# Two extra products of constants ahead of each pair of gathered tiles in the second gather's loop

## The chip, the cores and the metric

One NeuronCore of a Trainium2 chip runs the whole kernel as one launch. The metric is the device time of one execution in microseconds (us). The engines are named as in the profile: PE is the matrix engine (PEld its weight loads), DVE the vector engine, ACT the scalar engine, POOL the GpSimd engine that issues the gathers, and SP the sync engine. A difference of under 2% is about what a measurement of this kernel can't tell from no change.

## The reference, cut to what matters

```python
N_NODES, N_EDGES, D = 6250, 100000, 256
h    = layernorm(x) @ W.T                   # (6250, 256)
msgs = edge_weight[:, None] * h[dst]        # one row of 256 for each edge
x    = x + segment_sum(msgs, src, 6250)     # graph part: the gathers
x    = x + moe_ffn(layernorm(x))            # 16 experts, the best 2 of each node, F = 512
```

The edges come in the order of `dst`, so the kernel has to sort them by `src`, the node that a message is summed into. It sums the normalized rows first and multiplies the sums by W afterwards.

## The kernel before

The 6250 nodes are taken as 49 windows of 128 rows. The edges are sorted by window into tiles of 128 edges. For a tile, POOL gathers 128 rows of 256 numbers from DRAM (`xn_rows`) into SBUF by an indirect DMA, DVE builds a 128-wide table `picks` that holds each edge's weight in the column of its node, and PE multiplies the two, which adds the tile's messages to the window's sum in a PSUM bank.

There are two gathers. The first takes 4 tiles for each window (`fbuf`, lines L737, L1095, L1261) while the sort of the edges goes on. The second, which the change touches, takes the rest, in pairs of tiles:

- POOL (`gather_gpsimd`, L470) gathers a pair as two indirect DMAs of 128 rows into one of 16 places of `hbuf`. It needs the rows' numbers (`ix`, which DVE writes for half a ring, 8 pairs, at a time, L420, semaphore `ix_set`) and a free place (`used`, which PE raises).
- DVE (`gather_vector`, L491) builds `picks` for a pair, twice 128x256, in one of two buffers. It waits until PE has used the pair before last (`used`). At the third pair of each half ring it writes the numbers of the next half ring, and that releases POOL's next 16 gathers.
- SP (`gather_sync`, L456 to L458) waits for each pair's `picks` and for its gathers, and raises `pair_in`.
- PE (`gather_tensor`, L549) waits for `pair_in` and makes the pair's two products of 256 columns in fp32. Each is two MATMUL and two LDWEIGHTS records in the trace. `quad` does two pairs; `window` runs it in a loop over the window's quads, in which `used` is raised, and once more after the loop for the quad that the window shares with the next, in which it isn't: the next window begins with that same quad. Behind it come the transposes of the window before (`turn`, L558), the multiplication by W (`project`, L565 to L567) and the sum that the first gather left (L581), which opens the next window. ACT copies each closed window out (`agg`, L627) and works on the projected rows (L609 to L621).

After the gathers come the routing and the expert layers on all engines (from 1820 us on in the trace), and a last normalization. In them PE works with the same banks, after the gathers' end. Bank 6 is used by nothing in the second gather.

What each line does in the loop is seen in the code. `s` counts pairs, `q` is the window's bank and half of `picks`:

Of the kernel before, what the change touches and what calls it, by code (L numbers as in the profile page):

```python
# [18 lines left out]
def await_turn(engine, sem, turn, per, value):  # L19

    if isinstance(turn, int):
        if per * turn + value > 0:
            engine.wait_ge(sem, per * turn + value)
    else:
        engine.wait_ge(sem, turn * per + value)


def gnn_moe_kernel(nc, x, src, dst, edge_weight, gnn_w, gate_w, gate_b, w1, b1, w2, b2, gamma, beta, out):
# [4 lines left out]
    P = 128  # L33
# [62 lines left out]
    with ctx:  # L96
        def sb(name, shape, dt):
            return ctx.enter_context(nc.sbuf_tensor(name, shape, dt))

        def bank(name, shape, dt=fp32):  # L100
            return ctx.enter_context(nc.psum_tensor(name, shape, dt))
# [5 lines left out]
        ident = sb("ident", [P, P], fp32)  # L107
        iota_i = sb("iota_i", [P, P], i32)
        iota_two = sb("iota_two", [P, 2 * P], fp32)
# [176 lines left out]
        bk = [bank(f"bank{i}", [P, 512]) for i in range(8)]  # L286
# [140 lines left out]
        def window_pairs(engine, window):  # L427
            for w in range(4):
                window(w, w % 2)
            with engine.Fori(2, NW // 2) as i:  # L430
                window(i * 2, 0)
                window(i * 2 + 1, 1)
            window(NW - 1, 0)
# [107 lines left out]
            choose(SOON[1], NW)  # L541

        def gather_tensor(pe):
            def quad(s, q):
                place = s & (PR - 1)
                for j in range(2):
                    pe.wait_ge(pair_in, s + j)
                    for k in range(2):
                        m = nc.tensor.matmul(bk[q][:, 0:D], picks[:, j, k, q * P:(q + 1) * P],  # L549
                                             hbuf[:, ds(place + j, 1), k, :].rearrange("p s d -> p (s d)"),  # L550
                                             start=False, stop=False, skip_group_check=True)
                    yield m

            def turn(w, q):
                pe.wait_ge(agg_ready, w + 1)
                await_turn(pe, aggT_ready, w, 1, -1)
                for b in range(NB):
                    s = nc.tensor.transpose(bk[2 + q][:, b * P:(b + 1) * P], agg[q][:, b * P:(b + 1) * P], ident[:])  # L558
                s.then_inc(agg_turned, 1)

            def project(w, q):
                pe.wait_ge(aggT_ready, w + 1)
                await_turn(pe, x1_added, w, 1, -1)
                for b in range(NB):
                    nc.tensor.matmul(bk[4 + q][:, 0:D + EX], aggT[q][:, b, :], wT[:, b, :], start=b == 0, stop=False, skip_group_check=True)  # L565
                nc.tensor.matmul(bk[4 + q][:, D:D + EX], ident[:], raw[:, ds(w, 1), :].rearrange("p w e -> p (w e)"), start=False, stop=False, skip_group_check=True)
                s = nc.tensor.matmul(bk[4 + q][:, 0:D], ident[:], x1[:, ds(w, 1), :].rearrange("p w d -> p (w d)"), start=False, stop=True, skip_group_check=True)  # L567
                s.then_inc(projected, 1)

            def window(w, q):  # L570
                first = pe.value_load(quad_i[0:1, ds(w, 1)], min_val=1, max_val=TT // 2)
                end = pe.value_load(quad_i[0:1, ds(w + 1, 1)], min_val=3, max_val=TT // 2)
                if isinstance(w, int) and w == 0:
                    pe.wait_ge(rows_in[0], 32)
                if isinstance(w, int) and 2 <= w < 4:
                    for t in range(w - 1, WT - 1) if w == 3 else (1,):
                        pe.wait_ge(rows_in[t], 32)
                    if w == 3:
                        pe.wait_ge(rows_in[WT - 1], 48)
                await_turn(pe, agg_ready, w, 1, -1)  # L580
                nc.tensor.matmul(bk[q][:, 0:D], ident[:], first_sums[:, ds(w, 1), :].rearrange("p w d -> p (w d)"), start=True, stop=False, skip_group_check=True)  # L581
                with pe.Fori(first, end, 2) as s:
                    for m in quad(s, q):
                        m.then_inc(used, 1)

                for m in quad(end, q):
                    pass
                m.then_inc(closed, 1)
                if not isinstance(w, int) or w >= 1:
                    turn(w - 1, 1 - q)  # L590
                if not isinstance(w, int) or w >= 2:
                    project(w - 2, q)

            pe.wait_ge(tables_ready, FBLK + TBLK)
            pe.wait_ge(first_summed, NW)
            pe.sem_inc(used, PR)
            window_pairs(pe, window)

            pe.wait_ge(closed, NW)
            pe.sem_inc(used, 2 * PR)  # L600
            turn(NW - 1, 0)
            project(NW - 2, 1)
            project(NW - 1, 0)
# [1324 lines left out]
```

## Time and profile before

| | |
|---|---|
| time, median of 3 runs | 2383.14 us (2364.69 to 2874.64) |
| time of the profiled execution | 2405.79 us |
| its span, first to last instruction | 2404.0 us |
| granted PE clock over the span | 0.787 of 2.4 GHz |
| second gather, 625 to 1820 us | 1195 us |
| PE busy in it | 641.0 us, at a granted clock of 0.74 |
| POOL busy in it | 614.9 us, 640 gathers |

The second gather is half of the span. A granted clock of 0.74 is a mean over stretches at 1.2 GHz (0.5) and stretches at 2.4 GHz (1.0). No engine is busy for more than 54% of this half, so the time lies in what they wait for from each other.

### The profile page before, as it was taken

How to read it: one execution, taken by the hardware profiler on the slowest of the kernel's cores; microseconds unless marked ns; L12 is line 12 of the kernel's file. 1: busy time of each engine (PE TensorE's matmuls, PEld its weight loads, DVE VectorE, ACT ScalarE, POOL GpSimd, SP SyncE). 2: the span in 40 equal slices, each digit the busy share in tenths (PEclk: the TensorE clock that was granted, in tenths of full speed). 3: DMA queues.
4: the chain of work that ended last, by engine and by line, in shares of the span. 5: the costliest groups of instructions: out<-in, count | busy, mean ns of one | idle time of the engine just before them, and what ended most of it. 6: DMA issues, size and time to landing. Idle time of an engine off the chain costs nothing. (4 is left out here: it accounts for less than half of the span.)

```text
span 2404.0 us, 33977 instructions
## 1 busy us (share of the span) xinstructions
PE 1508.3 (63%) x7875; PEld 1206.6 (50%) x7876; DVE 970.1 (40%) x2547; ACT 645.8 (27%) x1788; POOL 1204.3 (50%) x1170
## 2 busy tenths in 40 slices
PE   5256977564445565555565546464644799998975
PEld 3245866452334343333343434343433799897864
DVE  7995799472112222222222132121317333332338
ACT  5741266330000110101010100101015344443456
POOL 0045558786655555555555444545552355454434
PEclk9595589686668676877677767677876999999988
DMA  4112212224522222222222222222236222224346
GB/s 154 62 54 82 77 52 66 72 66 142 179 79 72 70 70 70 70 70 70 70 70 70 70 61 65 72 66 74 72 70 190 86 71 77 94 85 159 118 145 229
DMA packets 121466, 215.63 MB, mean 90 GB/s; under 512 B 21001, under 2 KB 82756, under 8 KB 121281
## 3 DMA queue, kind: packets, MB, share of 16 engines
q0 software_dynamic: 52864, 140.45, 19.9%
q1 hardware_dynamic: 53664, 56.14, 7.0%
q10 hardware_dynamic: 14880, 18.35, 2.3%
q8 instruction: 26, 0.43, 0.1%
q14 instruction: 32, 0.25, 0.0%
HBM read 172.32 MB, written 42.54 MB: 89 GB/s over the span
## 5 line engine op out<-in xcount | busy, mean ns | idle before, releaser
L470 POOL DMA_INDIRECT hbuf<-xn_rows,ix x640 | 614.9, 961 | 574.2 <-DVE ix L420 217.8
L549 PE MATMUL bank<-hbuf,picks 128*128 x1640 | 535.1, 477 | 549.8 <-SPq L458 274.4
L549 PEld LDWEIGHTS bank<-hbuf,picks 128*128 128x128 f32 x1640 | 363.6, 237 | 714.1 <-issue 660.4
L491 DVE TENSOR_SCALAR picks<-iota_two,marks 128x256 f32<-128x256 f32 x640 | 239.5, 420 | 920.6 <-remote 616.4
L737 POOL DMA_INDIRECT fbuf<-xn_rows,first_tables x196 | 230.1, 1174 | 130.0 <-PE bank L1261 66.9
L627 ACT ACTIVATE agg<-bank 128x256 f32<-128x256 f32 x49 | 18.8, 385 | 863.3 <-PE bank L549 565.5
L1845 PE MATMUL bank<-rowsT,w_sb 128*128 128x128 f32 x1744 | 216.3, 278 | 19.1 <-issue 19.1
L1845 PEld LDWEIGHTS bank<-rowsT,w_sb 128*128 128x128 f32 x1744 | 212.2, 193 | 31.0 <-issue 26.3
L1855 PE MATMUL bank<-w_sb,hT 128*128 128x256 f32 x872 | 209.2, 382 | 0.9 <-ACT hT L1803 0.6
L1781 POOL DMA_INDIRECT expert_out<-y_sb,to_i x112 | 111.4, 995 | 192.6 <-DVE y_sb L1890 188.0
L1279 PE MATMUL bank<-work 128*128 128x192 bf16 x1568 | 154.8, 254 | 75.2 <-DVE work L1067 57.1
L1279 PEld LDWEIGHTS bank<-work 128*128 128x128 bf16 x1568 | 137.8, 99 | 97.8 <-issue 95.1
L1803 ACT ACTIVATE hT<-bank,b_cols 128x128 f32<-128x128 f32 x436 | 139.6, 366 | 164.4 <-PE bank L1845 152.6
L1261 PE MATMUL bank<-fbuf,x 128*128 128x256 f32 x392 | 149.2, 506 | 48.9 <-DMA fbuf<-xn_rows,first_tables 22.9
L1855 PEld LDWEIGHTS bank<-w_sb,hT 128*128 128x128 f32 x872 | 157.6, 191 | 20.1 <-ACT hT L1803 2.7
L726 POOL DMA_INDIRECT edge_groups<-recs,dest_i x56 | 85.2, 1521 | 162.1 <-DVE recs L1074 143.2
L1771 POOL DMA_INDIRECT xt<-xn_rows,from_i x116 | 112.9, 973 | 68.6 <-issue 36.7
L1261 PEld LDWEIGHTS bank<-fbuf,x 128*128 128x128 f32 x392 | 84.5, 246 | 68.8 <-issue 34.8
L1890 DVE TENSOR_TENSOR y_sb<-bank,b_b 128x256 f32 x109 | 46.3, 425 | 167.0 <-PE bank L1855 162.2
L1095 DVE TENSOR_SCALAR x<-iota_two,first_tables 128x128 f32<-128x128 f32 x196 | 65.2, 367 | 119.2 <-PE bank L1261 53.2
L1067 DVE TENSOR_TENSOR work<-work,tables 128x768 bf16<-128x768 bf16 (+2 forms) x176 | 95.5, 599 | 5.6
L1051 DVE TENSOR_TENSOR work<-iota_rows,low_i 128x512 bf16<-128x512 bf16 (+2 forms) x136 | 95.1, 749 | 0.2 <-DVE tables L1146 0.2
(293 smaller groups left out, 1729.0 us busy)
## 6 DMA issues: line engine op xcount, KB each, us to landing
w_sb<-in_L_ffn_w_dram ACTq DMA_DIRECT2D x28, 512.0 KB
hbuf<-xn_rows,ix POOLq DMA_INDIRECT x640
first_sums<-x SPq DMA_DIRECT2D x49, 128.0 KB
first_sums_back<-first_sums SPq DMA_DIRECT2D x7, 896.0 KB
xn_rows<-xn SPq DMA_DIRECT2D x7, 896.0 KB, 4.6
x<-in_x_dram SPq DMA_DIRECT2D x6, 896.0 KB
ya<-expert_out SPq DMA_DIRECT2D x5, 896.0 KB, 5.3
yb<-expert_out SPq DMA_DIRECT2D x5, 896.0 KB, 7.2
```

Of the source, the lines that this page charges most:

```text
L470: pool.indirect_dma_start(hbuf[:, 1 + j, k, :], None, xn_dram, bass.IndirectOffsetOnAxis(ap=ix[:, 2 * j + k:2 * j + k + 1], axis=0)).then_ ...
L491: s = v.tensor_scalar(picks[:, j % 2, k, :], iota_two[:], marks[:, 0, 2 * j + k:2 * j + k + 1], marks[:, 1, 2 * j + k:2 * j + k + 1], ALU. ...
L549: m = nc.tensor.matmul(bk[q][:, 0:D], picks[:, j, k, q * P:(q + 1) * P], hbuf[:, ds(place + j, 1), k, :].rearrange("p s d -> p (s d)"), st ...
L737: pool.indirect_dma_start(fbuf[:, s % RH, :], None, xn_dram, bass.IndirectOffsetOnAxis(ap=fdst_i[:, s:s + 1], axis=0)).then_inc(xn_gathere ...
L1067: s = v.tensor_tensor(fields[n % RM][:, h0:h1, :, :, :], colhot[n % RJ][:, h0:h1, None, :, :].to_broadcast(shape), pieces[:, e0 + h0:e0 + ...
L1261: nc.tensor.matmul(bk[w % 2][:, 0:D], fpicks[:, used % RK, :], fbuf[:, used % RH, :], start=t == 0, stop=t == FT - 1).then_inc(first_used, 1)
L1279: s = nc.tensor.matmul(sums_at[c % 2][h][:, 0:2 * PIECES * SP_], rowhot[n % RP][:, k // 2, h * P:(h + 1) * P, k % 2], fields[n % RM][:, k ...
L1771: pool.indirect_dma_start(xt[:, k, :], None, xn2_dram, bass.IndirectOffsetOnAxis(ap=from_i[:, k:k + 1], axis=0)).then_inc(xt_in[k], 16)
L1781: pool.indirect_dma_start(y_dram, bass.IndirectOffsetOnAxis(ap=to_i[:, k:k + 1], axis=0), y_sb[:, k % 2, :], None).then_inc(y_sent[k], 16)
L1803: act.activation(hT[:, f, :], bk[f][:, 0:P], ACT.Relu, bias=b1_cols[:, ds(e * FB + f, 1)]).then_inc(hT_ready, 1)
L1845: m = nc.tensor.matmul(bk[f][:, 0:P], w1_sb[:, q, b, f * P:(f + 1) * P], rowsT[:, b, :], start=b == 0, stop=b == NB - 1)
L1855: m = nc.tensor.matmul(bk[5][:, 0:D], hT[:, f, :], w2_sb[:, q, f, :], start=f == 0, stop=f == FB - 1)
```

## The change

Inside the loop over a window's quads, and not in the quad behind it, PE makes two further products for each pair, after its wait for `pair_in` and ahead of the pair's own two. Both multiply the identity by `iota_two`, a constant of 256 columns, in fp32, into bank 6. Nobody reads that bank, and no semaphore is raised by them.

```diff
-            def quad(s, q):
+            def quad(s, q, kept_busy):
                 place = s & (PR - 1)
                 for j in range(2):
                     pe.wait_ge(pair_in, s + j)
+                    if kept_busy:
+                        for k in range(2):
+                            nc.tensor.matmul(bk[6][:, 0:2 * P], ident[:], iota_two[:], start=True, stop=True)
                     for k in range(2):
                         m = nc.tensor.matmul(bk[q][:, 0:D], picks[:, j, k, q * P:(q + 1) * P],
...
-                    for m in quad(s, q):
+                    for m in quad(s, q, True):
                         m.then_inc(used, 1)
 
-                for m in quad(end, q):
+                for m in quad(end, q, False):
                     pass
```

PE is the only engine whose instructions change. This is its queue from the first window's opening sum through one turn of the loop, before. A REGISTER_ALU on line 549 carries the wait for `pair_in`, and the ISA rows set up addresses:

```order
L581 MATMUL bank<-first_sums_back,ident 128x256
L582 UNCONDITIONAL_BRANCH
L549 REGISTER_ALU
L549 ISA
L549 MATMUL bank<-hbuf,picks 128x256
L549 ISA
L549 MATMUL bank<-hbuf,picks 128x256
L547 REGISTER_ALU
L549 ISA
L549 MATMUL bank<-hbuf,picks 128x256
L549 ISA
L549 MATMUL bank<-hbuf,picks 128x256
```

The same place now. Lines from 547 on have moved down by three:

```order
L584 MATMUL bank<-first_sums_back,ident 128x256
L585 UNCONDITIONAL_BRANCH
L550 MATMUL bank<-iota_two,ident 128x256 x2
L552 REGISTER_ALU
L552 ISA
L552 MATMUL bank<-hbuf,picks 128x256
L552 ISA
L552 MATMUL bank<-hbuf,picks 128x256
L547 REGISTER_ALU
L550 MATMUL bank<-iota_two,ident 128x256 x2
L552 ISA
L552 MATMUL bank<-hbuf,picks 128x256
```

The two products stand at the head of each pair, and now the first of them carries the wait for `pair_in`. The address instructions come behind them.

## Rows read from the trace of the kernel before

**Rows 1.** The page's head: busy time, share of the span, instructions.

```profile
span 2404.0 us, 33977 instructions
PE 1508.3 (63%) x7875; PEld 1206.6 (50%) x7876; DVE 970.1 (40%) x2547; ACT 645.8 (27%) x1788; POOL 1204.3 (50%) x1170
```

**Rows 2.** Windows: three stages; columns in the first row.

```profile
core 0: us, PE busy (x) PEld busy (x) DVE busy (x) ACT busy (x) POOL busy (x), PEclk, DMA share, GB/s
0.00:625.00 625.00, 384.80 (x2515) 312.39 (x2516) 449.26 (x1005) 261.76 (x608) 320.65 (x273) 0.75 0.29 89
625.00:1820.00 1195.00, 641.00 (x2228) 456.62 (x2228) 265.64 (x732) 114.20 (x441) 614.88 (x640) 0.74 0.25 71
1820.00:2404.00 584.00, 482.48 (x3132) 437.62 (x3132) 255.18 (x813) 269.86 (x739) 268.72 (x257) 0.93 0.39 128
```

**Rows 3.** Groups by line: busy us, mean ns, then idle before, by releaser.

```profile
L470 POOL DMA_INDIRECT hbuf<-xn_rows,ix x640 | 614.9, 961 | 574.2 <-DVE ix L420 217.8 <-issue 197.7 <-PE bank L549 158.4
L549 PE MATMUL bank<-hbuf,picks 128*128 x1640 | 535.1, 477 | 549.8 <-SPq L458 274.4 <-issue 273.5
L491 DVE TENSOR_SCALAR picks<-iota_two,marks 128x256 f32<-128x256 f32 x640 | 239.5, 420 | 920.6 <-remote 616.4 <-PE bank L549 246.2 <-issue 44.4
```

**Rows 4.** Timeline, POOL, 1209 to 1263 us: gathers at bursts' starts and ends.

```profile
1209.49 0.95 POOL L470 DMA_INDIRECT hbuf<-xn_rows,ix  x1 [14.23 <-DVE ix L420]
1210.74 1.04 POOL L470 DMA_INDIRECT hbuf<-xn_rows,ix  x1 [0.30 <-issue]
...
1228.46 0.96 POOL L470 DMA_INDIRECT hbuf<-xn_rows,ix  x1 [0.30 <-issue]
1234.55 0.95 POOL L470 DMA_INDIRECT hbuf<-xn_rows,ix  x1 [5.13 <-DVE ix L420]
```

**Rows 5.** Timeline, ACT and DVE, the same stretch.

```profile
1230.40 0.38 ACT L627 ACTIVATE agg<-bank 128x256 f32<-128x256 f32 x1 [22.00 <-remote]
1232.77 0.73 DVE L491 TENSOR_SCALAR picks<-iota_two,marks 128x256 f32<-128x256 f32 x2 [15.84 <-remote]
1233.42 0.17 DVE L420 COPY ix<-tables 128x16 int32 x1
```

**Rows 6.** Timeline, PE, the same stretch: runs of records, start and length.

```profile
1211.24 1.99 PE L549 MATMUL bank<-hbuf,picks 128*128 x8 [0.40 <-SPq L458]
1213.75 1.99 PE L549 MATMUL bank<-hbuf,picks 128*128 x8 [0.52 <-issue]
1216.41 1.99 PE L549 MATMUL bank<-hbuf,picks 128*128 x8 [0.67 <-issue]
1218.23 0.38 PE L558 MATMUL bank<-ident,agg 128*128 128x128 f32 x2
...
1224.65 2.07 PE L549 MATMUL bank<-hbuf,picks 128*128 x4 [1.44 <-issue]
1233.79 6.08 PE L549 MATMUL bank<-hbuf,picks 128*128 x16 [7.08 <-SPq L458]
```

**Rows 7.** Windows on `hbuf`, pauses between bursts: PE, PEld, POOL busy, clock, DMA.

```profile
1195.30:1209.50 14.20, 9.64 (x27) 6.99 (x28) 0.01 (x1) 0.70 0.03 10
...
1229.40:1234.50 5.10, 0.71 (x2) 0.63 (x3) 0.02 (x1) 0.50 0.09 29
...
1254.50:1262.70 8.20, 4.03 (x11) 3.18 (x12) 0.02 (x1) 0.54 0.06 16
...
1282.80:1291.10 8.30, 5.56 (x15) 4.09 (x16) 0.00 (x0) 0.61 0.06 16
...
1311.00:1320.80 9.80, 7.73 (x19) 5.54 (x20) 0.00 (x0) 0.54 0.05 14
...
1340.90:1355.70 14.80, 8.19 (x24) 5.90 (x25) 0.02 (x1) 0.67 0.03 9
```

**Rows 8.** Source L549: durations in ns, min/median/max, first and last start.

```profile
L549 PE MATMUL bank<-hbuf,picks x1640: 379/379/792, 631.7 to 1811.6; 128*128 x183
```

**Rows 9.** Timeline, first gather, 599 to 618 us, PE and DVE.

```profile
599.73 5.85 PE L1261 MATMUL bank<-fbuf,x 128*128 128x256 f32 x18 [1.60 <-DVE x L1095]
618.03 0.35 DVE L1095 TENSOR_SCALAR x<-iota_two,first_tables 128x128 f32<-128x128 f32 x1 [11.91 <-PE bank L1261]
```

## The prediction

> **What bounds the kernel now.** I read the stages first, then the second gather by lines, then one turn of its ring in time. The stage that the change touches runs from 625 to 1820 us, 1195 of 2404 us [rows 1, 2]. Nothing is saturated in it: PE is busy for 641 us, POOL for 615, DVE for 266 [rows 2]. So the question is what each waits for. POOL sat idle for 574 us ahead of its 640 gathers: 198 us of it are "issue", the 0.30 us between two gathers, and 218 + 158 = 376 us are waits for the row numbers that DVE writes and for places that PE frees [rows 3].
>
> In time this is a ring with two phases. POOL gets 8 pairs' numbers at once and issues 16 gathers 1.26 us apart, so a burst takes 20 us (1209.5 to 1229.4). Then it pauses until DVE writes the next numbers (1233.42) and starts again at 1234.55 [rows 4, 5]. The 640 gathers make 40 such groups of 16, the first two in one go, so there are 38 pauses. The 376 us over 38 pauses are 9.9 us each, and 20 + 9.9 = 29.9 us for each turn, which over 39 bursts gives the stage's length. A burst can't be shorter unless POOL is, so **the pauses are what can grow or shrink**, and a pause ends when DVE has got two pairs past the half ring's start, which needs PE to have used the pairs before.
>
> What fills a pause? Its first part is a late hand-over. PE's records show a window's last quad at 1216.41 (8 records, 1.99 us), yet ACT, which needs nothing but that window's end, starts at 1230.40, and DVE, which needs the pair of the run at 1224.65 or before, only at 1232.77 [rows 5, 6]. Both move just after the burst's end at 1229.4. So in the later part of a burst what PE has finished becomes visible to the others only about when the burst ends. The rest of a pause is PE and DVE working through the remaining pairs. Six pauses in a row hold 27 + 2 + 11 + 15 + 19 + 24 = 98 records of L549, 16.3 or **4.1 pairs for each pause** (4 records make a pair), and these took 35.9 us of PE, 0.37 us a record, at granted clocks of 0.50 to 0.70 [rows 7]. The work in a pause runs mostly at 1.2 GHz, since PE has just stood still.
>
> **What the change adds.** L549 has 1640 records, 410 pair visits [rows 3]. The 49 closing quads are 98 of them and get nothing, so 312 visits get two more products, 4 more records each, 1248 records in all. A product has the shape of the pair's own (128x128 by 256 columns, fp32), so rows of L549 price it:
> - At 2.4 GHz a run of 8 records takes 1.99 us [rows 6]. The last record's own 0.38 us [rows 8] is in it, so records follow each other by 1.61 / 7 = 0.23 us, and 4 cost 0.92 us.
> - At 1.2 GHz 16 records take 6.08 us, partly after the clock had risen: 5.70 / 15 = 0.38 us apart, so 4 cost 1.5 us or a little more [rows 6].
>
> But a pair at 2.4 GHz does not cost PE's time now. The runs of 8 start 2.5 us apart (1211.24, 1213.75) for 1.99 us of work [rows 6], 1.25 us a pair; with 16 records for the two pairs PE would be busy for 16 x 0.23 = 3.7 us. The growth is **0.6 us a pair at 2.4 GHz**: the DVE table (0.73 us [rows 5]) and the hand-over hide behind the longer PE work. At 1.2 GHz PE is dense already (16 records without a gap), so nothing hides and the growth is 1.5 us or more. The address instructions that now stand behind the first product save something like a tenth or two of a microsecond at each pair's head; they lie beside PE's work, and I leave this out.
>
> Per pause: of 4.1 visits about 0.7 are closing ones without extra (98 of 410 visits are, fewer of them in pauses), so 3.4 get it. The first 4 to 5 us after PE's restart stay at 1.2 GHz: one pair and a half instead of two and a half. That is 1.5 x 1.5 = 2.3 us more for those, and the other two pairs grow by 0.6 each if they were at 2.4 GHz already, 1.2 us, together 3.5 us. The one pair that moves from the slow to the fast clock gives back about 0.4 (1.5 less the 0.92 and a little of the hand-over), so I take **3.1 us**. Over 38 pauses 3.1 x 38 = **118 us**.
>
> In the bursts: some 5 visits a turn lie before the late hand-over begins. Each becomes 0.6 us longer, but what follows waits for the burst's end anyway, so this costs nothing by itself. The cover is the burst's 20 us. Where PE crosses the window's end early in a burst, fewer pairs get done in it, and the rest move to the pause: I put 0.3 to 0.5 of a pair, 0.7 us, on each turn, 39 x 0.7 = 27 us. This is the term that I know least. From below it is nothing; from above all 312 visits lie open at 0.92 us (287 us) or at the mean price of a record in this stage, 535.1 / 1640 = 0.33 us, 1248 x 0.33 = 407 us [rows 3].
>
> The sum is 118 + 27 = 145 us on an execution of 2405.79 us, of which all but 1.8 is the span. That execution is 0.95% above the median of the runs, 2383.14; I add the same 145 us to the median: **2528 us**, 6.1% slower. No stage after 1820 us changes: PE's clock there is 0.93 already and its first tile waits for the routing.
>
> **The clock.** The rows say that PE in the stage has a granted clock of 0.74, and 0.50 to 0.70 in pauses [rows 2, 7], with the drop behind the long stand in the burst (1226.7 to 1233.8, [rows 6]). The extra products come after the wait for `pair_in`, so they run when the pair's own products could, and put nothing into the stand that lets the clock fall. The Trainium skill ("TensorE: Matmul & The Clock Gate", "What's actually happening") says that the idle PE is throttled to 1.2 GHz and that activity releases it, and that rule speaks for this change: more activity, more time at 2.4 GHz. What the rule gives here is the rival below, worked from rows; the trace agrees that the clock is low behind a stand, but not that work placed behind the wait would shorten the stand.
>
> **Rivals.**
> 1. *Nothing hides* (the late hand-over moves with PE's work instead of ending with the burst). Then all 312 visits cost 0.92 to 1.3 us, 287 to 407 us: 2670 to 2790 us; I take the lower end, since a PE that works more stands less. For it: the stand begins behind a window's end, a place in PE's own program. Against: ACT and DVE both woke 1 to 3 us after the burst ended [rows 4, 5].
> 2. *The clock pays for it.* If the extra work keeps PE at 2.4 GHz in the pauses, the records there cost 0.23 instead of 0.37 us: 98 records over six pauses give back 13.7 us, 2.3 us a pause, 87 us, against 3.4 x 0.6 x 38 = 78 us and the 27: within 20 us of no change, 2374 to 2401 us. It holds if the clock is at 2.4 GHz at each restart. Against: the stands.
> 3. *The late hand-over goes away: faster.* If what is late is late because PE's queue is short of work, a longer queue could carry the news through. With no stand, 8 pairs of 16 / 2 x 0.23 = 1.84 us and the closing work fit in the 20 us of a burst, and the pauses (376 us) go; half of that is 190 us, 2195 us. It decides when the pause falls below some 7 us a turn. Against: in the first gather PE ran 18 records in 5.85 us without a gap, a dense queue, and DVE still waited 11.91 us for it, until 618.03 [rows 9]. The Trainium skill ("Perfetto Trace Analysis", "Tensor Engine Instruction (MATMUL, LD_WEIGHTS)") says that a matmul's recorded end is an estimate and that the semaphore is raised later, once PSUM has acknowledged the write; the trace agrees that the two can lie apart, by up to 12 us here, and the sentence gives no price.
>
> **How the numbers follow.** The forecast has 0.55, rival 1 0.20, rival 2 0.15, rival 3 0.10. The predicted time is the forecast's, 2528. The range 2390 to 2700 holds the forecast with its unknown term, half of rival 2 and most of rival 1, about 0.80. A difference under 2% (2335 to 2431) is about what a measurement can't tell from none: it takes rival 2 and the low end of the forecast, 0.17. Faster by more is rival 3, 0.10; slower 0.73.
>
> **What the profile after would show.** The products on L550 with some 1248 records; still 16 gathers in 20 us; pauses of some 13 us instead of 9.9, so the idle time of POOL before L470 for DVE and PE near 500 us instead of 376; ACT and DVE still waking just after a burst's end; a stage of some 1335 us; a granted clock in it near 0.77. If the pauses stay near 10 us with bursts the same, the growth was hidden and the price of a pair in a pause is wrong; if a turn is shorter than a burst plus 5 us, the hand-over depends on PE's queue and rival 3 holds; if the stands last beyond a burst's end, it is rival 1. The forecast is wrong above all if the late hand-over is not tied to POOL's burst, which one trace can't settle.

## The result, and the profile after

| | before | after |
|---|---|---|
| median, same chip | 2385.49 us (4 runs, 2364.69 to 2874.64) | 2516.05 us (4 runs, 2494.24 to 2529.63) |
| profiled execution | 2405.79 us, span 2404.0 | 2494.24 us, span 2492.2 |

The ratio is 1.057, with a 95% interval of 1.045 to 1.069: the change makes the kernel slower by 131 us. Ratios and intervals here leave out executions in a slower state, such as the one of 2874.64 us, so that a ratio can differ a little from that of two medians. The forecast was 2528 us. The execution profiled after (2494.24 us) is the fastest of its four, and the one before (2405.79 us) lies above its median, so the spans are only 88 us apart. I therefore compare places, not spans.

The page's head, and the windows over the three stages (columns as in [rows 2]):

```profile
span 2492.2 us, 36473 instructions
PE 1733.8 (70%) x9123; PEld 1447.6 (58%) x9124; DVE 967.8 (39%) x2547; ACT 646.7 (26%) x1788; POOL 1206.7 (48%) x1170
```

```profile
0.00:601.00 601.00, 367.51 (x2515) 297.23 (x2516) 447.73 (x1003) 260.56 (x608) 324.23 (x273) 0.79 0.30 93
601.00:1910.00 1309.00, 883.41 (x3471) 712.13 (x3472) 263.98 (x729) 110.58 (x432) 613.76 (x640) 0.83 0.23 65
1910.00:2492.00 582.00, 482.89 (x3139) 438.21 (x3137) 256.05 (x815) 275.52 (x750) 268.73 (x257) 0.93 0.39 129
```

Against [rows 2] the second gather takes 1309 us instead of 1195, +114. PE is busy for 242 us more in it, POOL, DVE and ACT as before. The last stage is as it was (582 against 584). The first took 24 us less with the same 2515 matmul records, at a granted clock of 0.79 instead of 0.75; the change has no instruction there, so I take that as a difference between two executions. 114 - 24 - 2 makes the 88 us of the spans.

The groups by line in the second gather (busy, mean ns, idle before by releaser), which answer to [rows 3]:

```profile
L470 POOL DMA_INDIRECT hbuf<-xn_rows,ix x640 | 613.8, 959 | 686.6 <-PE bank L552 451.7 <-issue 187.8 <-DVE ix L420 46.8
L552 PE MATMUL bank<-hbuf,picks 128*128 x1640 | 474.4, 421 | 96.4 <-issue 71.8 <-SPq L458 24.6
L550 PE MATMUL bank<-iota_two,ident 128*128 128x256 f32 x1248 | 381.5, 434 | 326.6 <-SPq L458 210.2 <-issue 116.4
L491 DVE TENSOR_SCALAR picks<-iota_two,marks 128x256 f32<-128x256 f32 x640 | 237.9, 418 | 1038.8 <-remote 605.9 <-PE bank L552 407.2 <-issue 11.8
```

Read the first row's idle time: 451.7 + 46.8 = 498.5 us in the two waits that make the pauses, against 376.2 before, so 122 us more. With 10 us less under "issue" (187.8 against 197.7) that is the stage's growth. The name that dominates has changed from "DVE ix" to "PE bank", and this means nothing: by the code a gather needs the place of the pair 16 before it, which was free long ago, and in both traces each of the 38 bursts behind a pause starts 0.87 to 1.19 us after DVE has written its numbers. DVE's numbers end every pause, before and after. DVE's row separates two things. Its idle time under "remote", the news of PE that comes late, is 606 us against 616: nearly unchanged. Its idle time for PE's matmuls grew from 246 to 407 us. PE's own idle time under "issue", in which it waited for nothing that the profile shows, fell: 71.8 + 116.4 = 188 us against 273.5 [rows 3]. So the longer program did not wait more for its own instructions.

Now one turn of the ring, POOL first, then DVE and PE (start, length, idle before with its releaser):

```profile
1202.83 0.95 POOL L470 DMA_INDIRECT hbuf<-xn_rows,ix  x1 [14.13 <-PE bank L552]
...
1221.75 0.95 POOL L470 DMA_INDIRECT hbuf<-xn_rows,ix  x1 [0.30 <-issue]
1240.02 0.95 POOL L470 DMA_INDIRECT hbuf<-xn_rows,ix  x1 [17.32 <-PE bank L552]
```

```profile
1222.76 0.73 DVE L491 TENSOR_SCALAR picks<-iota_two,marks 128x256 f32<-128x256 f32 x2 [9.73 <-remote]
...
1238.33 0.73 DVE L491 TENSOR_SCALAR picks<-iota_two,marks 128x256 f32<-128x256 f32 x2 [5.66 <-PE bank L552]
1238.98 0.17 DVE L420 COPY ix<-tables 128x16 int32 x1
1240.06 0.73 DVE L491 TENSOR_SCALAR picks<-iota_two,marks 128x256 f32<-128x256 f32 x2 [0.91 <-PE bank L552]
```

```profile
1214.22 1.03 PE L552 MATMUL bank<-hbuf,picks 128*128 x4
1223.60 2.07 PE L550 MATMUL bank<-iota_two,ident 128*128 128x256 f32 x4 [8.35 <-issue]
1225.47 1.91 PE L552 MATMUL bank<-hbuf,picks 128*128 x4
1227.17 1.91 PE L550 MATMUL bank<-iota_two,ident 128*128 128x256 f32 x4
1228.88 1.09 PE L552 MATMUL bank<-hbuf,picks 128*128 x4
...
1237.92 1.03 PE L550 MATMUL bank<-iota_two,ident 128*128 128x256 f32 x4
1238.79 1.03 PE L552 MATMUL bank<-hbuf,picks 128*128 x4
```

The burst is the same, 16 gathers from 1202.83 to 1222.70. PE's last records in it end at 1215.25 (1214.22 + 1.03), and then it stands for 8.35 us. DVE, which waits for one of PE's pairs, wakes at 1222.76, 7.5 us after that pair was done, and at the burst's end. The trace also records when the semaphore `used` was raised for that pair: at 1222.53, 7.3 us after the pair's recorded end. DVE was not slow to wake; the raise itself is late. Only then does the pause's work begin, and it is slower at both clocks. After the stand runs of four start 1.7 to 1.9 us apart (1223.60, 1225.47, 1227.17, 1228.88), and every second run is constants. Later they start 0.865 us apart, so a pair takes 1.73 us; DVE's tables at 1238.33 and 1240.06 show the same 1.73. POOL restarts at 1240.02.

Six pauses in a row, in windows:

```profile
1188.70:1202.80 14.10, 10.26 (x34) 8.56 (x35) 3.88 (x13) 0.00 (x0) 0.00 (x0) 0.66 0.03 10
1222.70:1240.00 17.30, 16.09 (x62) 13.13 (x63) 4.49 (x13) 2.31 (x9) 0.00 (x0) 0.82 0.03 8
...
1353.60:1366.40 12.80, 10.52 (x42) 9.08 (x43) 4.50 (x13) 0.00 (x0) 0.07 (x2) 0.80 0.04 10
sum 78.10, PE 61.20 PEld 50.74 DVE 21.33 ACT 6.88 POOL 0.11; mean PE 10.20 PEld 8.46 DVE 3.55 ACT 1.15 POOL 0.02
```

78.1 / 6 = 13.0 us for each, the same as 498.5 / 38 = 13.1 over the whole stage, against 9.9 before. The granted clock in them is 0.66 to 0.82, where it was 0.50 to 0.70 [rows 7]. The pauses also hold more pairs: over windows on all 38 of them, 676 records of the pairs' products against 604 before, 4.4 pairs a pause instead of 4.0. Some pairs have moved out of the bursts.

### The profile page after: what moved, and what is told of

The parts are those of the page before. It is cut to its first block and busy times, and to the rows that moved or that the text cites. A ratio compares the mean times of both kernels' runs of the same rounds, so it can differ in the third digit from the quotient of the medians.

```text
span 2492.2 us, 36473 instructions
## 1 busy us (share of the span) xinstructions
PE 1733.8 (70%) x9123; PEld 1447.6 (58%) x9124; DVE 967.8 (39%) x2547; ACT 646.7 (26%) x1788; POOL 1206.7 (48%) x1170
## 5 line engine op out<-in xcount | busy, mean ns | idle before, releaser
L470 POOL DMA_INDIRECT hbuf<-xn_rows,ix x640 | 613.8, 959 | 686.6 <-PE bank L552 451.7
L550 PE MATMUL bank<-iota_two,ident 128*128 128x256 f32 x1248 | 381.5, 434 | 326.6 <-SPq L458 210.2
L552 PE MATMUL bank<-hbuf,picks 128*128 x1640 | 474.4, 421 | 96.4 <-issue 71.8
L550 PEld LDWEIGHTS bank<-iota_two,ident 128*128 128x128 f32 x1248 | 265.0, 218 | 394.7 <-SPq L458 225.1
L552 PEld LDWEIGHTS bank<-hbuf,picks 128*128 128x128 f32 x1640 | 344.7, 213 | 175.5 <-issue 119.8
L740 POOL DMA_INDIRECT fbuf<-xn_rows,first_tables x196 | 239.0, 1220 | 106.5 <-issue 50.7
L1264 PE MATMUL bank<-fbuf,x 128*128 128x256 f32 x392 | 137.3, 470 | 71.6 <-DMA fbuf<-xn_rows,first_tables 27.1
L729 POOL DMA_INDIRECT edge_groups<-recs,dest_i x56 | 79.8, 1424 | 163.6 <-DVE recs L1077 145.0
L1264 PEld LDWEIGHTS bank<-fbuf,x 128*128 128x128 f32 x392 | 77.6, 225 | 92.8 <-issue 44.3
```

The source lines that it names most:

```text
L470: pool.indirect_dma_start(hbuf[:, 1 + j, k, :], None, xn_dram, bass.IndirectOffsetOnAxis(ap=ix[:, 2 * j + k:2 * j + k + 1], axis=0)).then_ ...
L550: nc.tensor.matmul(bk[6][:, 0:2 * P], ident[:], iota_two[:], start=True, stop=True)
L740: pool.indirect_dma_start(fbuf[:, s % RH, :], None, xn_dram, bass.IndirectOffsetOnAxis(ap=fdst_i[:, s:s + 1], axis=0)).then_inc(xn_gathere ...
L1264: nc.tensor.matmul(bk[w % 2][:, 0:D], fpicks[:, used % RK, :], fbuf[:, used % RH, :], start=t == 0, stop=t == FT - 1).then_inc(first_used, 1)
```

## The experiments

The kernels of each group below ran on one chip, beside the kernel before on that chip, and each ratio is taken within its group. This matters: the kernel before takes 1960 to 1980 us on the chips of the first two groups (its medians there are 1979.28 and 1959.56) and 2383.85 us on the chip of the third, which is the time of the first measurement (2385.49). I call the last kind "a chip with stands": on it PE stands idle in each turn until its late news has arrived. All expectations of the first group were worked for such a chip.

### Group 1: the dose, the width and the place

One product for each pair instead of two:

```diff
-                        for k in range(2):
+                        for k in range(1):
                             nc.tensor.matmul(bk[6][:, 0:2 * P], ident[:], iota_two[:], start=True, stop=True)
```

> One extra product for each pair instead of two, half the dose. Theory (the extra time lies in POOL's pauses, where a pair's growth is what exceeds the 1.25 us that the hand-over with DVE takes anyway): a product is 2 records of 0.23 us at 2.4 GHz, so a pair takes 1.38 us of PE instead of 1.84 us and grows by some 0.15 us at the fast clock and 0.76 us at the slow one; pauses of 11 us, 1.5 to 2.5% over the kernel before, less than half of what two products cost (5.7%). Rival (every product lies open, nothing hides): cost in proportion, 2.8% or more.

Measured: 1977.77 us, ratio 1.003 (0.997 to 1.010).

Four products:

```diff
-                        for k in range(2):
+                        for k in range(4):
                             nc.tensor.matmul(bk[6][:, 0:2 * P], ident[:], iota_two[:], start=True, stop=True)
```

> Four extra products for each pair, the double dose. Theory: now PE is the bound in every pair (12 records of 0.23 us, 2.8 us), no slack is left, so the next two products cost more than the first two: pauses of 17 to 18 us, 12 to 15% over the kernel before. The late hand-over still ends with POOL's burst of 20 us. Rival (proportional): 11.5%. Rival (a fuller PE queue makes the late hand-over go away): under 8%.

Measured: 2215.90 us, ratio 1.128 (1.115 to 1.141).

Two products of 16 columns:

```diff
-                            nc.tensor.matmul(bk[6][:, 0:2 * P], ident[:], iota_two[:], start=True, stop=True)
+                            nc.tensor.matmul(bk[6][:, 0:16], ident[:], iota_two[:, 0:16], start=True, stop=True)
```

> Two extra products for each pair as in the change, but of 16 columns instead of 256: the same instructions, semaphores and loads of weights, little array time. Theory (array time counts): like half the dose or less, since a record of 16 columns behind a weight load follows in 0.11 us instead of 0.23 us: 1 to 2.5% over the kernel before. Rival (what costs is the number of PE instructions, fetched or issued late while POOL issues gathers): as much as the change, 5 to 6%.

Measured: 1969.75 us, ratio 1.003 (0.996 to 1.009).

Both full products ahead of the wait, where they could run in the stand:

```diff
-                    pe.wait_ge(pair_in, s + j)
                     if kept_busy:
                         for k in range(2):
                             nc.tensor.matmul(bk[6][:, 0:2 * P], ident[:], iota_two[:], start=True, stop=True)
+                    pe.wait_ge(pair_in, s + j)
```

> The same two products of 256 columns, placed ahead of the wait for the pair instead of behind it. Theory: PE makes those of the first pair during its stand, which saves 1.5 us at each restart, and hides some 0.3 us of each hand-over; 3.5 to 5% over the kernel before. Rival (position is nothing, PE's total work counts): 5.7% as the change. Rival (work during the stand keeps the clock at 2.4 GHz and pays for itself): within 1% of the kernel before.

Measured: 1969.61 us, ratio 0.9995 (0.994 to 1.005).

Three of the four cost nothing that can be measured. The fourth came out at my theory's size, but for another reason, as the next rows show. POOL's wait ahead of L470 in the kernel with four products (line waited for: us, times, longest), and its window over the second gather:

```profile
POOL hbuf L470 <- DVE ix L420: 252.0, 37, 18.1
```

```profile
561.00:1617.00 1056.00, 1020.06 (x4692) 874.12 (x4692) 261.91 (x712) 107.10 (x417) 614.94 (x639) 0.99 0.28 80
```

Here PE is busy for 1020 of 1056 us at a granted clock of 0.99: it bounds the stage. DVE's tables for two pairs follow each other by 2.59 us (1205.10, 1207.69), 20.7 us for 8 pairs, and the window's closing work comes on top, against 20.2 us for POOL's 16 gathers. With one product POOL waits for DVE and PE only 4.9 + 2.4 = 7.3 us in the whole stage, and the stage is 820 us long. So on this chip my theory had no ring with pauses to act on, and the dose, width and place tell nothing about one.

### Group 2: before and after, on a chip without stands

The kernel before, for its trace:

> The kernel before, unchanged, for its trace on the chip of this call. The first four experiments ran where the kernel before takes 1979 us, not 2385. If the difference is the late hand-over, the pauses of POOL and the stands of PE of about 10 us must be gone where the time is near 1980 us, and there where it is near 2385 us.

Measured: 1956.76 us in one run. The change itself:

> The change itself, unchanged, beside the kernel before on the chip of this call. Theory (extra PE time costs only where POOL has to wait for PE): where the kernel before takes 1980 us, POOL issues without a pause, 8 pairs take it 20 us, and PE with 1.84 us for a pair and the closing work needs 18 to 20 us: no more than 1% slower. Where it takes 2385 us: 5 to 6.5% slower, as first measured. Rival (the cost of the change is its own PE time everywhere): 5% or more in both.

Measured: 1969.50 us, ratio 1.003 (0.998 to 1.008). One product again:

> One extra product for each pair, again, now with the change itself beside it. Theory: nothing where the kernel before takes 1980 us (1.003 was measured there); where it takes 2385 us, 1.5 to 2.5% slower, less than half of what two products cost. Rival (nothing hides): half of the change's cost.

Measured: 1964.50 us, ratio 1.002 (0.998 to 1.007).

The windows over the second gather, before and then after, each a kernel of its own; and of each the rows by line of POOL's gathers and DVE's tables:

```profile
560.00:1380.00 820.00, 597.50 (x2228) 429.61 (x2228) 282.45 (x744) 114.18 (x441) 618.16 (x640) 0.88 0.36 104
```

```profile
L470 POOL DMA_INDIRECT hbuf<-xn_rows,ix x640 | 618.2, 966 | 199.8 <-issue 185.4 <-PE bank L549 8.6 <-DVE ix L420 5.8
L491 DVE TENSOR_SCALAR picks<-iota_two,marks 128x256 f32<-128x256 f32 x640 | 251.1, 436 | 525.3 <-PE bank L549 507.5 <-PEq L600 7.0 <-DVE marks L482 2.3
```

```profile
561.00:1383.00 822.00, 761.88 (x3476) 642.66 (x3476) 273.27 (x728) 112.55 (x439) 618.78 (x640) 0.98 0.36 103
```

```profile
L470 POOL DMA_INDIRECT hbuf<-xn_rows,ix x638 | 617.0, 967 | 206.9 <-issue 184.3 <-PE bank L552 17.4 <-DVE ix L420 5.2
L491 DVE TENSOR_SCALAR picks<-iota_two,marks 128x256 f32<-128x256 f32 x639 | 245.8, 427 | 540.7 <-PE bank L552 537.2 <-PEq L603 1.7 <-DVE marks L482 1.0
```

The same kernel before, another chip: POOL's gathers take as long (966 ns, with 185 us of "issue" beside 198), but the 376 us of waits [rows 3] are 14.4 us here, and DVE's 616 us under "remote" are gone. Nothing arrives late, and POOL alone sets the stage, 820 us. The change then adds 164 us to PE's busy time (762 instead of 598) and 2 us to the stage. PE has 19.0 us of work for each of the 40 half rings of 20.5 us, so it fits, barely: POOL's waits grew by 8 us. The two chips' records also differ in the register instructions on the queues of PE and SP, between the products and waits. Here are one of the loop over a window's quads, on the queue of PE's weight loads, and one of SP's. First the chip of the first measurement, then this one (duration ns as min/median/max):

```profile
L582 PEldq ALU_OP  x155: 2/32/711, 632.5 to 1797.2; - x155
L454 SPq ALU_OP  x285: 5/33/729, 692.9 to 1815.8; - x143
```

```profile
L582 PEldq ALU_OP  x155: 32/32/32, 567.7 to 1351.7; - x155
L454 SPq ALU_OP  x285: 32/33/52, 605.0 to 1378.1; - x143
```

On the chip with stands some of these take 0.7 us where they take 32 ns otherwise, and one of L549 takes 1.425 us where none takes over 0.060 here. They are not spread evenly. In the trace of the first measurement 62 register instructions on PE's queue in this stage take over 0.65 us; all of them start 7.9 us or more after the start of one of POOL's bursts, and 60 lie inside a burst. SP's 8 such lie inside bursts too. DVE's and ACT's queues have none. The semaphores differ as well: on this chip every raise of `used` and `closed` by PE is recorded 0.02 us or less after the product's end. So on the chip with stands two things happen during a burst, mostly in its later part: PE's and SP's queues run slowly, and PE's raises come late. Whether one causes the other isn't shown.

The last of the group keeps POOL 8 pairs further behind PE than the ring needs, to break its bursts up:

```diff
-                    await_turn(pool, used, i, PR, j + 1)
+                    await_turn(pool, used, i, PR, j + 1 + 8)
```

> The kernel before with no extra products, but POOL may gather at most 8 pairs ahead of PE instead of 16, so that a burst of 16 gathers is broken up when PE stands. If PE's news is late because POOL issues gathers without a break, a stand ends some gathers earlier and the stage gets shorter where the kernel before takes 2385 us: 3 to 10% faster. Rival (the stand has another cause): the same time or slower, since the gathers start later. Where it takes 1980 us POOL is the bound: within 2%.

Measured: 1959.41 us, ratio 1.002 (0.996 to 1.008). Where nothing comes late there is nothing for it to mend, so it settles nothing.

### Group 3: on a chip with stands

Three products (`range(3)` in place of `range(2)`), on a chip that proved to be of the first measurement's kind; the expectation was worked for the other:

> Three extra products for each pair. One and two cost nothing where the kernel before takes 1960 to 1980 us, four cost 12.8%. Theory (the cost starts where PE's work for 8 pairs passes the 20.4 us that POOL needs for their 16 gathers): in a half ring stand 7.8 loop visits of 10 records of 0.23 us, 17.9 us, 2.4 closing visits of 0.92 us, 2.3 us, and 1.2 windows' transposes and projections of some 2.5 us, 3 us: 23 us, 2.8 us over POOL's, 40 times, 112 us: 4.5 to 7% slower. For two the same sum gives 19.7 us, just under it. Rival (a smooth cost): 1 to 3%.

Measured: 2632.32 us, ratio 1.106 (1.099 to 1.112). POOL's waits:

```profile
POOL hbuf L470 <- DVE ix L420: 596.5, 37, 24.7
POOL hbuf L470 <- issue: 189.9, 574, 14.7
POOL hbuf L470 <- PE bank L552: 21.9, 28, 12.5
```

618 us, 16.3 us for each pause. With no, two and three products the pauses are 9.9, 13.1 and 16.3 us, and the kernel is 0, 5.7 and 10.6% slower. The first two cost 131 us together and the third 116 to 121, so it costs nearly twice their mean. DVE's tables now follow each other by 2.16 us (0.43 us more than with two). 3.4 visits a pause at 0.43 would be 1.5 us, not 3.2, so some of the work moved out of the burst into the pause. The windows on the 38 pauses show how much: 782 records of the pairs against 676, 0.7 of a pair more for each pause, which at 2.16 us a pair is the other 1.5 us.

The other three put a stand of known length into the kernel. Behind each closed window ACT makes 20 copies, one after the other, and PE waits for the last before it goes on with the window before:

```diff
                 m.then_inc(closed, 1)
+                pe.wait_ge(stand, w * 20 + 20)
...
                 act.activation(agg[q][:], bk[q][:, 0:D], ACT.Copy).then_inc(agg_ready, 1)
+                for k in range(20):
+                    act.activation(spent2[:], iota_two[:], ACT.Copy).then_inc(stand, 1)
+                    act.wait_ge(stand, w * 20 + (k + 1))
```

> The kernel before with a stand built in, no extra products: behind each window's close ACT makes 20 copies of a constant, one after the other, and PE waits for the last, 9 to 10 us in which PE has nothing to do. It imitates what PE met behind each window in the first measurement, 49 times. Theory: the stands put PE on the path again and its clock falls in each: 2350 to 2500 us where the kernel before takes 1960, ratio 1.20 to 1.28.

Measured: 2597.93 us, ratio 1.092 (1.085 to 1.099). The expectation had been worked for a chip without stands, from 1960 us; here the new stand met the one that was there. The timeline of a turn on ACT, PE and DVE:

```profile
1211.73 8.91 ACT L631 ACTIVATE spent<-iota_two 128x256 bf16<-128x256 f32 x20
1220.69 0.69 PE L559 MATMUL bank<-ident,agg 128*128 128x128 f32 x2 [9.39 <-ACT spent L631]
...
1225.08 1.89 PE L550 MATMUL bank<-hbuf,picks 128*128 x8
1230.46 1.38 DVE L492 TENSOR_SCALAR picks<-iota_two,marks 128x256 f32<-128x256 f32 x4 [20.50 <-remote]
```

49 stands of 8.9 us are 436 us, and the time grew by 214: half of them was covered. That they lay where PE's news would have been late anyway is my reading; it agrees with DVE's idle time under "remote", 484.5 us here against 616.4. In the turn shown PE goes on at 1220.69 and has its next two pairs done by 1226.97 (1225.08 + 1.89), and DVE wakes at 1230.46, past the end of the burst that began at 1207.61.

The same with the change's two products in the loop:

> The same stand with the change's two products for each pair. Theory (they cost when PE is on the path, 0.6 us a pair at the fast clock and 1.5 us at the slow one after each stand): 312 x 0.6 = 187 us and some 50 us for the slow restarts, 8 to 12% over the kernel with the stand alone. Rival (the change costs nothing here, as it did without a stand): equal to it. Rival (the activity keeps the clock up and pays): under 4% over it.

Measured: 2851.43 us, ratio 1.195 (1.187 to 1.203); against the kernel with the stand alone 253.5 us or 9.8% slower. And the stand filled: no products in the loop, but 20 behind each window's last quad, ahead of the wait for the stand:

```diff
                 m.then_inc(closed, 1)
+                for k in range(20):
+                    nc.tensor.matmul(bk[6][:, 0:2 * P], ident[:], iota_two[:], start=True, stop=True)
                 pe.wait_ge(stand, w * 20 + 20)
```

> The same stand, no products in the loop, but 20 of the same products of constants between a window's close and the wait for ACT, 9 us of PE work inside the stand. Theory (products help the clock only where PE would stand): PE leaves the stand at 2.4 GHz, which saves 1.5 to 2.5 us of each restart, 75 to 120 us: 3 to 5% under the kernel with the stand alone. Rival (the clock is worth nothing): the same time; or slower by what the products stick out of the stand.

Measured: 2662.41 us, ratio 1.118 (1.111 to 1.125), 2.5% slower than the stand alone, where 3 to 5% faster was expected. The windows over the second gather, of the stand alone, the stand with the change, the stand filled:

```profile
606.00:1981.00 1375.00, 667.45 (x2176) 493.71 (x2176) 254.48 (x702) 506.32 (x1377) 610.57 (x640) 0.73 0.21 61
```

```profile
618.00:2248.00 1630.00, 918.24 (x3408) 738.37 (x3408) 256.19 (x702) 506.48 (x1377) 609.62 (x640) 0.74 0.18 52
```

```profile
609.00:2041.00 1432.00, 1043.34 (x4096) 806.58 (x4096) 255.84 (x702) 502.28 (x1369) 610.90 (x640) 0.87 0.21 59
```

With the stand, the change costs 255 us of stage, 0.82 us for each of the 312 visits. That is nearly what four records take back to back at 2.4 GHz (0.865 us above), so almost nothing of it is hidden once PE has less time to work in. The filled stand raises the granted clock of the stage from 0.73 to 0.87. What did it buy? The pair's own products and the projection (L566), which stands right behind the stand, in the stand alone and in the filled one:

```profile
L550 PE MATMUL bank<-hbuf,picks 128*128 x1616 | 466.1, 440 | 199.7 <-SPq L459 175.7 <-issue 23.5
L566 PE MATMUL bank<-wT,aggT 128*128 128x272 f32 x184 | 93.0, 661 | 0.0
```

```profile
L550 PE MATMUL bank<-hbuf,picks 128*128 x1616 | 466.3, 438 | 202.3 <-SPq L459 150.0 <-issue 50.9
...
L591 PE MATMUL bank<-iota_two,ident 128*128 128x256 f32 x1920 | 440.6, 384 | 81.6 <-issue 81.3
L566 PE MATMUL bank<-wT,aggT 128*128 128x272 f32 x184 | 62.0, 469 | 0.0
```

The pairs' products gained nothing: 440 and 438 ns. The products that close a window did, since they come directly after the stand: the projection's records took 469 instead of 661 ns. All five lines of this work (L559, L566 to L568, L582) were busy for 179 us instead of 246, 1.4 us less for each window, nearly the 1.5 to 2.5 us that were expected. The rest of the higher mean clock is the filler's own. Yet the stage is 57 us longer. In some windows the filler stuck out of the stand, as PE's timeline shows:

```profile
1217.29 7.93 PE L591 MATMUL bank<-iota_two,ident 128*128 128x256 f32 x36
1226.13 0.38 PE L591 MATMUL bank<-iota_two,ident 128*128 128x256 f32 x1 [0.91 <-issue]
...
1232.45 0.58 PE L591 MATMUL bank<-iota_two,ident 128*128 128x256 f32 x1 [1.53 <-issue]
1233.85 0.68 PE L559 MATMUL bank<-ident,agg 128*128 128x128 f32 x2 [0.82 <-issue]
```

36 records take 7.93 us, and the last four come 2.1 us apart with nothing recorded to wait for. The chain behind them starts at 1233.85, though ACT's copies, which PE waits for, began at 1218.83 and took 8.92 us. So the fill made this stand 6.1 us longer, and 3.4 of them lie in POOL's burst (1211.26 to 1231.11). This turn is not the common one. In 37 of 48 windows the chain starts within 0.13 us of ACT's last copy, as it does in all 48 without the fill; in 11 it starts 3.2 to 7.2 us after it, 63 us in all. That is about the stage's growth, so the 67 us that the work behind the stand gained shortened nothing; where it was covered was not separated.

## Why the prediction was right, and where it was not

**The ring and its pauses: right.** 16 gathers still take 20 us, and the growth lies in the pauses: 13.1 us each for a predicted 13, 498.5 us of waits for "near 500". The sum of 145 us was too high by 14 us on the medians and by 31 us on the profiled stage (114 us). That 2528 lies only 12 us from the median measured is in part luck: the four executions after spread over 35 us, and for the stage the sum was off by 31.

**The late hand-over: right for this chip, wrong in what it belongs to.** "Remote" stayed at 606 us and DVE woke at the burst's end, as predicted. I read the late news as a trait of this kernel. The second group shows the same kernel without it, in 1960 us. On that chip the same edit costs 0.3%, no more than can be measured, because POOL's gathers, which hardly pause there, cover PE's work. Whether this change costs anything depends on the chip.

**The price of a pair: near.** 0.6 us of growth at the fast clock was expected, from 1.25 to 1.84 us; 1.73 us was measured, a growth of 0.48. At the slow clock 1.5 us for four records was expected, and 1.7 was seen (1225.47, 1227.17, 1228.88). The two errors partly cancel in 3.1.

**The in-burst term of 27 us: seen, at about its size.** It was the term that the prediction knew least: 0.3 to 0.5 of a pair would move from each burst into the pause, 0.7 us a turn. The 38 pauses hold 72 more of the pairs' records, 18 pairs, 0.47 a pause. At 1.25 to 1.73 us a pair that is 23 to 31 us. It is part of the 122 us of POOL's waits.

**The term of 118 us: too large by a fifth to a quarter.** What is left of the 122 us is 91 to 99 us, 2.4 to 2.6 us for each pause instead of 3.1. The growth of 0.48 us a pair instead of 0.6 explains part of it.

**The clock: direction right, size not.** I put the stage's clock at 0.77, and it was 0.83. More activity did mean more time at 2.4 GHz. The Trainium skill ("TensorE: Matmul & The Clock Gate", "What's actually happening") says that activity releases the throttle, and the traces agree (0.74 before, 0.83 after). But what the pairs' records gained (477 to 421 ns each [rows 3], 60.7 us in all) is a sixth of what the constants took (381.5 us). Not all of it is the clock: at 2.4 GHz the first record of a run shows some 478 ns and the next 379, and the first is now a constant.

**The rivals.** Rival 1 (nothing hides, 2670 to 2790 us) is refuted by the 122 us; the stand with the change shows that it is the right price once the slack is gone, 0.82 us a visit. Rival 2 (the clock pays) is refuted by the size of the growth on a chip with stands. Rival 3 (the late news goes away) is refuted by "remote", 616 and 606 us.

**What stays open.** Why PE's news is late, and its queue slow, on one chip and not on another. The later part of POOL's bursts is the stretch in which it happens, but on the other chips POOL gathers without a break and nothing is late, so the gathers alone don't do it. The kernel that was to break the bursts up ran there too, so it isn't shown that they play a part. One product, narrow products and products ahead of the wait weren't run on a chip with stands; their cost there is not known. No version here beat the kernel before by more than can be measured.

## What to carry to other kernels

Work that is put behind a wait can't keep an engine warm through that wait; it lengthens the part that others wait for, by its own time less the slack of the nearest pacer. Work that is put into the stand itself can bring the instructions right behind it to the faster clock, but it must fit in the stand every time: here it stuck out in 11 windows of 48, and the stage got longer by about as much. A higher mean clock must be checked against the duration of the useful instructions, since most of it may be the filler's own. Before a cost is carried over, compare the idle time under "remote" between chips: the same edit cost 5.7% where a late signal had already used up the cover, and 0.3% where none did.

## What the runs showed of the hardware

- The same kernel took 2384 to 2385 us in the first measurement and on the third group's chip, and 1960 to 1980 us on the chips of the other two groups. The instructions' own times agree (a gather 961 and 966 ns); the profiled spans differ by 449 us, 375 of them in the second gather (1195 against 820 us), where POOL waits 376 us on the one and 14 on the other, 65 ahead of it and 9 behind it.
- On the slower chip the raise of a semaphore by PE's last product was recorded 7.3 us after that product's end in the turn shown; on a chip without stands every one came within 0.02 us. In the kernel before, the raise for a window's end was recorded at 1230.22, 11.8 us after the end of the last product of the quad at 1216.41 [rows 6].
- On the slower chip register instructions on PE's queue took up to 1.425 us (one of L549, at most 0.060 otherwise), 60 of the 62 over 0.65 us inside POOL's bursts and none earlier than 7.9 us after a burst's start; on DVE's and ACT's queues none took over 0.081 us on either chip.
- A product of 128x128 by 256 fp32 columns is two records, 0.216 us apart in a dense queue at 2.4 GHz (0.865 / 4) and 0.43 us at 1.2 GHz (1.7 / 4).
- POOL's indirect gather of 128 rows of 1 KB costs it 0.96 us and 0.30 us to the next, 1.26 us, on every chip traced; this is the floor of the second gather, 640 x 1.26 = 806 us of the 820.
